# Attention pass of a macaron block: couplings, inverse products and reads in halves of eight heads, slot sums taken out of PSUM, new engine orders with four tiles in flight

## The reference

```
x = x + 0.5 * ffn(layernorm(x))
x = x + attn(layernorm(x))
x = x + 0.5 * ffn(layernorm(x))

attn(x):  q, k = l2norm(x@Wq), l2norm(x@Wk);  v = x@Wv
          a = sigmoid(x@Wa + ba);  b = sigmoid(x@Wb + bb)        # one number per head
          for every token: pred = S^T k;  S = a*S + k (b*(v - pred))^T;  y = S^T q
          return (rmsnorm(y, g_norm) * silu(x@Wg)) @ Wo
ffn(x):   logits = (gelu([x, mean(slots)]@w1.T + b1)@w2.T + b2) / (|tau| + 0.1)
          alpha  = softmax over the 8 greatest of 64 logits, 0 elsewhere
          slots' = GRU(alpha^T x / sum(alpha), slots);  return (alpha @ (slots'@wv.T + bv))@wo.T + bo
```

## Time and profile before

| | |
|---|---|
| median of 3 runs | 3262.46 us (3257.69 to 3265.82) |
| profiled execution, its own time | 3255.6 us |
| its span, first to last instruction | 3253.7 us |
| PE / DVE / POOL / ACT busy | 87% / 60% / 38% / 29% of the span |
| mean granted TensorE clock | 0.94 |
| attention pass begins | about 331.6 us from the span's start |

### The profile page before, as it was taken

How to read it: one execution, slowest core, us unless ns; L and a number is a source line. 1 busy time by engine, 2 the same in 40 slices (tenths; PEclk the granted TensorE clock), 3 DMA queues, 4 the chain that set the end, 5 groups by cost and what they waited for, 6 DMA issues and landing times.

```text
span 3253.7 us, 121458 instructions
## 1 busy us (share of the span) xinstructions
PE 2816.3 (87%) x52828; PEld 1973.8 (61%) x52828; DVE 1939.1 (60%) x5299; ACT 944.0 (29%) x1634; POOL 1232.0 (38%) x1608
## 2 busy tenths in 40 slices
PE   6998778898988888888888888898988898889857
PEld 5786456565666665666666556666666665666643
DVE  6776446565666665666655556565656666655635
ACT  4775122222222222222222222222222222222210
POOL 2221344344444443444444434443444443444400
PEclk9999899999999999999999999999999999999978
DMA  6341122221212222222122221122222222112167
GB/s 207 98 151 48 34 55 56 49 56 30 54 50 56 56 55 56 56 56 56 49 50 56 56 49 44 37 53 56 56 56 56 56 56 56 52 48 56 49 213 287
DMA packets 365983, 225.05 MB, mean 69 GB/s; under 512 B 277584, under 2 KB 294032, under 8 KB 365456
## 3 DMA queue, kind: packets, MB, share of 16 engines
q1 hardware_dynamic: 356240, 200.51, 22.6%
q10 hardware_dynamic: 9216, 16.78, 1.4%
HBM read 125.49 MB, written 74.97 MB: 62 GB/s over the span
## 4 chain that ended last, share of the span: by engine, by line
PE 49%; DVE 32%; issue 10%; DMA 4%; SPq 2%; POOL 1%; ACT 1%; DVEq 0%; POOLq 0%; ACTq 0%
DVE blk L1823 12%; DVE blk L1825 12%; PE psum L784 8%; PE psum L958 5%; PE psum L867 4%; PE psum L938 4%; PE psum L915 4%; PE psum L885 4%; PE psum L925 4%; PE psum L829 3%; DMA xin<-in_L_attn_x_dram 3%; PE psum L852 2%; PE psum L898 2%; PE psum L986 2%; PE psum L778 2%
## 5 line engine op out<-in xcount | busy, mean ns | idle before, releaser
L784 PE MATMUL psum<-w_kvqg,xnT 128*128 128x512 f32 x1536 | 730.7, 609 | 5.2 <-issue 2.0
L1369 POOL TENSOR_TENSOR sm<-sm,half 128x1 f32<-128x1 f32 (+1 forms) x384 | 518.2, 1350 | 476.8 <-DVE sm L1765 198.1
L1823 DVE TENSOR_TENSOR blk<-blk 128x30 f32<-128x30 f32 (+14 forms) x960 | 379.9, 396 | 84.9 <-issue 53.0
L784 PEld LDWEIGHTS psum<-w_kvqg,xnT 128*128 128x128 f32 x1536 | 271.4, 191 | 257.1 <-issue 229.8
L1825 DVE TENSOR_TENSOR blk<-blk 128x30 f32<-128x30 f32 (+14 forms) x960 | 375.8, 391 | 33.0
L1403 POOL TENSOR_SCALAR sm<-sm 128x1 f32<-128x1 f32 x64 | 14.6, 228 | 772.6 <-DVE sm L1733 772.6
L829 PE MATMUL psum<-xnT,w_kvqg 128*128 128x128 f32 x2048 | 300.1, 309 | 0.0
L829 PEld LDWEIGHTS psum<-xnT,w_kvqg 128*128 128x128 f32 x2048 | 289.6, 224 | 17.2 <-issue 17.2
L958 PE MATMUL psum<-w_out,gate 128*128 128x512 f32 x512 | 265.4, 643 | 2.9 <-issue 1.3
L1841 DVE STREAM_TRANSPOSE st<-psum 128x128 f32<-128x128 f32 x256 | 80.9, 316 | 278.2 <-PE psum L938 277.8
L1199 ACT ACTIVATE xn<-xc,sm 128x512 f32<-128x512 f32 x64 | 52.0, 813 | 657.5 <-POOL sm L1407 657.5
(11 more groups left out here) (271 smaller groups left out, 4839.2 us busy)
## 6 DMA issues: line engine op xcount, KB each, us to landing
blk<-n_scratch SPq DMA_DIRECT2D x64, 512.0 KB, 4.9
xin<-in_L_attn_x_dram SPq DMA_DIRECT2D x96, 256.0 KB, 2.9
n_scratch<-nn SPq DMA_DIRECT2D x64, 256.0 KB, 3.3
xh<-xc SPq DMA_DIRECT2D x64, 256.0 KB, 2.5
e_scratch<-blk SPq DMA_DIRECT2D x32, 512.0 KB, 2.6
E<-e_scratch SPq DMA_DIRECT2D x64, 256.0 KB, 4.3
x_scratch<-xh SPq DMA_DIRECT2D x62, 256.0 KB, 4.5
rxn<-in_L_attn_x_dram SPq DMA_DIRECT2D x32, 256.0 KB, 3.1
```

What stands on the lines that cost most here:

```text
L784: last = mm(dst, xnT[b][:, k * P:(k + 1) * P], w_kvqg[:, (k * 4 + m) * D:(k * 4 + m + 1) * D], start=(k == 0), stop=(k == KC - 1))
L1369: return g.tensor_tensor(dst, a, half[:, 0:n], ALU.pow)
L1823: own(tt(o, Y[:, 0:rows, s_:s_ + 1].to_broadcast([P, rows, cols]), N[:, s_:s_ + 1, s_ + 1:CH].to_broadcast([P, rows, cols]), ALU.mult))
```

## The change

All of it is in the attention pass, but for one scaling of Wo.

- **Halves.** `gram`, `coupling`, `reading`, `apply_uw`, `move_uw`, `qe_T`, `apply_gy`, `move_gq` and `chunk_kept` work on halves of eight heads, each half in one PSUM bank of its own. `apply_gy` goes through four pieces of two turns; each turn has 8 products where it had 16, and is awaited before the next on the same bank.
- **Projections.** Value and gate-decay columns stand side by side: `proj_va` takes the 32 columns of Wa and Wb and the first 256 of Wv, `proj_vb` the other 256. `ab` is gone. The values are kept in two places by turns (`vk` has three parts).
- **cum.** 32 products per tile with 4 columns become 4 products with 32 columns; DVE prepares their operand `glx`.
- **Gate.** ScalarE computes Silu at once; before it took Tanh and DVE finished it. The factor 0.5 in `set_out` goes. `y_mean` moves from DVE to ScalarE. The four `max(.,1e-24)` of the norms move from DVE to POOL.
- **Slot sums.** `slots` starts and stops in one bank; ScalarE copies it out (`slot_copy`), POOL adds it to `slotacc` (`slot_add`). Before, a bank of its own summed over all tiles.
- **Orders and depth.** Four tiles are in flight (p, q, r, s), over 35 steps where there were 34. The bank map and all five orders are new. The couplings of a tile are now made in the step after its projections, and inverted in the same step; `apply_uw` of b = 0 ends that step.

The core of the diff:

```diff
-        gram_at = [banks(3, 2), banks(5, 2)]
-        uw_at = [banks(1, 2), banks(4, 2)]
-        gq_at = [banks(4, 2), banks(4, 2)]
-        slot_at = banks(7, 1)
+        slot_at = banks(1, 1)
+        gram_at = [[banks(7, 1), banks(6, 1)], [banks(1, 1), banks(3, 1)]]
+        uw_at = [[banks(7, 1), banks(3, 1)], [banks(1, 1), banks(4, 1)]]
+        gq_at = [[banks(6, 1), banks(5, 1)], [banks(2, 1), banks(5, 1)]]
...
+            def proj_va(n, b):
+                pe.wait_ge(S["xnT"], both(n, b))
...
+                project(b, W_AB, 2 * H + D // 2, va_at[b][:, 0:2 * H + D // 2], range(KC)).then_inc(S["va_ps"], 1)
...
-                for b in range(B):
-                    for h in range(H):
-                        last = mm(q32(cum_at, h % NC, (6 + b) * H + h // NC * NC, NC),
-                                  gla[:, b * H + h:b * H + h + 1].to_broadcast([P, HD]),
-                                  chunk[:, 0:P:CH], start=False, stop=True, skip_group_check=True)
+                for hq in range(NC):
+                    last = mm(q32(cum_at, hq, 6 * H, 2 * H), ones[:, 0:HD], glx[:, hq * 2 * H:(hq + 1) * 2 * H],
+                              start=False, stop=True, skip_group_check=True)
...
+                for r in (2 * (piece % 2), 2 * (piece % 2) + 1):
+                    turn = 2 * NC * (n - 1) + NC * part + r
+                    since(gq_turn[b], turn)
                     stand_alone(pe)
...
+                    for k in range(2):
+                        for c in range(NC):
+                            hq = (c + r) % NC
+                            at = ((2 * part + k) * NC + hq) * 2 * HD
+                            last = mm(q32(gq_at[b][part], hq, (k * NC + c) * 2 * HD, 2 * HD), q32(uw[b], c, at + HD, HD),
+                                      q32(pk[b], c, at, 2 * HD), start=False, stop=True, skip_group_check=True)
+                    last.then_inc(gq_turn[b], 1)
+                    since(y1_turn[b], turn)
...
-            def tanh_g(n, b):
+            def gate_of(n, b):
                 sc.wait_ge(S["g_ps"], both(n, b))
...
+                act(gate[b][:, :], g_at[b], ACT.Silu).then_inc(S["gate"], 1)
...
+            def slot_copy(n):
+                sc.wait_ge(S["slot_ps"], both(n, 1))
+                since(S["sla"], n - 1)
+                act(slt[:, :], slot_at, ACT.Copy).then_inc(S["slc"], 1)
...
             def key_power(n, b):
                 pl.wait_ge(S["ssk"], both(n, b))
+                stand_alone(pl)
+                own(g.tensor_scalar(s(b, "ssk"), s(b, "ssk"), 1e-24, None, ALU.max))
...
+            def slot_add(n):
+                pl.wait_ge(S["slc"], n)
+                since(S["sla"], n - 1)
+                g.tensor_tensor(slotacc[:, 0:D], slotacc[:, 0:D], slt[:, :], ALU.add).then_inc(S["sla"], 1)
```

More of the change, by code:

```diff
@@ L119, in build @@
         gt = sb("gt", 28 * H)
+        slt = sb("slt", D)
+        glx = sb("glx", NC * B * H)
+        vk3 = [vk[b][:, :].rearrange("p (m h e) -> p m h e", m=3, h=H) for b in range(B)]
         def heads(t, n=1):
@@ L542, in drain_loads @@
             def drain_loads():
-                sp.wait_ge(y1_turn, NC * both(NT, 1))
+                for b in range(B):
+                    sp.wait_ge(y1_turn[b], 2 * NC * NT)
                 for g in range(3):
@@ L790, in proj_k @@
                     pe.wait_ge(S["xnT"], both(n, b))
-                    if b == 1:
-                        free((n, (S["zi"], n)))
-                last = project(b, 0, k_at[b], part)
+                    if b == 0:
+                        free((n - 2, (S["yv"], both(n - 2, 1))), (n - 1, (T["pt"][0], nth(n - 1, 0))))
+                    else:
+                        free((n - 2, (S["top"], both(n - 2 + NT, 0))), (n - 1, (S["vb"], both(n - 1, 1))))
+                last = project(b, W_K, D, k_at[b], (2 * part, 2 * part + 1))
                 if part == 1:
@@ L944, in y_norm @@
                 if b == 0:
-                    free((n, (S["qg"], both(n, 1))))
+                    free((n, (S["ysq"], both(n, 0))))
                 else:
@@ L1487, in step_pool @@
                     y_power(r, 1)
-                if p is not None:
-                    first_rstd(p, 0)
+                if q is not None:
+                    query_decayed(q, 0)
+                if s is not None:
+                    slot_add(s)
                 if r is not None:
@@ L1785, in key_turn @@
             def key_turn(n, b):
-                since(S["gram_ps"], both(n - 1, b))
+                since(T["gram_ps"][b], 2 * (n - 1))
                 ve.wait_ge(S["kn"], both(n, b))
@@ L1952, in step_dve @@
-                if q is not None:
-                    second_sum(q, 0)
-                    state(q, 1, 2)
-                    last_moments(q, 0)
-                    state(q, 1, 3)
-                    gated(q, 1)
-                if p is not None:
-                    coupling(p, 1)
+                    gates_beta(p)
             ve.wait_ge(wih_st, RELOAD)
```

900 lines of the change are left out of this document (476 added, 424 removed).

## The result

| | before | after |
|---|---|---|
| median, same chip | 3264.14 us (3257.69 to 3268.61, 4 runs) | 3332.66 us (3330.19 to 3355.88, 4 runs) |
| ratio | | **1.0235** (1.0206 to 1.0265) |
| profiled execution's own time, and its span | 3255.6, 3253.7 us | 3330.19, 3328.4 us |
| mean granted clock | 0.94 | 0.934 |
| step of the pass | 86.7 us | 88.3 us |

What follows compares the result with a forecast made beforehand. PE was taken to bound the kernel: 71.2 us work plus 4.3 us new waits make a 75.5 us step. 3255.6 - 31 x (86.7 - 75.5) + 13 for head and tail gave 2920 us; 8-in-10 range 2800 to 3065.

Steps and rivals of the forecast that it cites:

- Step of 86.7 us, and its split: One step on PE before the change: 10.0 us idle, at most 4.3 lost to low clock, 72.4 work.
- the wait of `logits`: PE's `logits` waits for `xc` from `first_sum(p,1)`, behind DVE's inversion: 4.97 us a step, half the idle time.
- the low clock with the gap: PE's 1.2 GHz level behind the `logits` gap, 4.4 us, claimed to go when that gap goes.
- Turns of `apply_gy` are half as long ... I take +0.3 (0 to 1): PE's shorter `apply_gy` turns: 0 to 0.06 us in each of 16 turns, +0.3 us a step taken.
- The work of 71.2 us: PE's full-clock work per new step: 72.4 - 1.3 (`ab`) - 0.35 (`cum`) + 0.3 (turns) + 0.2 (mode changes).
- The waits that go: On PE, the 4.97 us gap of `logits` and the low clock behind it go, barring a new gap that long.
- Waits that come: Four late places in the new order: 0.7, 0.6, 1.3 and 1.7 us, adding 4.3 us a step on PE.
- `uw` for `kn`: PE's `uw(r,1,0)` waits for `kn` because POOL's `key_power(q,1)` is late: 0.7 us a step.
- `first_sum(p,0)` holding the ring: DVE's `first_sum(p,0)` waits inside the inversion for `hold(q,0)`: 3 us in the ring, 1.7 us on PE at `chain(r,1,2)`.
- The ring of 70.4 us: Loop of PE work, couplings, DRAM trip, DVE inversion and inverse's return: 70.4 us, 74.7 with waits, just under PE's 75.5.
- The rival "slower": Loop through DVE, POOL, ScalarE and SP's queue over 11.6 us late, at `first_sum(p,0)`: 3300 us; chance 0.06.
- My own test: Signs of being wrong on PE include clock staying at 0.95 or `apply_gy` turns taking over 0.6 us.

Runs made afterwards that it cites:

- b1: Kernel before with `first_sum` and `first_moments` of b = 1 moved from behind the inversion to its middle: 3324.52 us, ratio 1.0153.
- a6: Kernel after without the counter increments in its apply products, waits kept: 3076.75 us, ratio 0.9397 to the kernel before.
- m4_which: TensorE alone, sets of 128 small and 6 big products, waits and increments varied separately: 10.8 us a set with 16 waits, 14.0 with 16 increments.
- m1_supply: TensorE alone, small products unbroken or alternating with big ones, some beside DRAM copies: unbroken, 1.99 us of work, then 1.5 to 1.7 us of nothing.
- m3_cover: TensorE alone, six stretches varying hand-overs and the products between them: full turns 11.0 us a set, halves 15.3, no hand-over 11.2.
- m2_turns: TensorE alone, small products with and without loads beside them, and sets in full or half turns: 10.5 us a set full, 15.6 in halves.

## Why the prediction was wrong

- **Step of 86.7 us, and its split: read rightly,** but the idle 10.0 us were then treated as if they were the wait of `logits` and small change. Of them 4.1 us are pauses inside runs of small products, released by nothing. They were there to be read in the kernel before, and no part of the change takes them away: even without the increments 3.9 us a step are left. To give back the low clock with the gap was nearly right: of the 38 stretches at the low level between 700 and 3000 us, 26 lie behind a wait of `logits`, with 195 of 235 us. What I took for nothing is the low clock behind other pauses, and these grew.
- **"Turns of `apply_gy` are half as long ... I take +0.3 (0 to 1)": the step that failed.** The hand-over itself was priced well (the half turns without increments cost 86.4 - 85.8 = 0.6 us a step in the kernel before). What I didn't count is that every turn carries an increment, so that 14 a step become 32. The half turns as they stand cost 96.6 - 86.7 = 9.9 us a step in the kernel before, where I took 0.3 and at most 1. In the kernel after the increments cost 88.3 - 80.4 = **7.9 us a step**: idle 2.4, low clock 2.8, and 2.7 of what the split calls work. The rows show a part of this last: at the full clock a pair of half turns takes 0.61 us with increments (1586.94 to 1587.55) and 0.51 without (1555.80 to 1556.31), 1.6 us for the 16 pairs of a step.
- **The work of 71.2 us: right but for the increments.** With them it is 74.0, without them 71.3. So `ab` into the value projection, `cum` and the mode changes were sized well together; none was tried alone.
- **"The waits that go": right** for `logits`. That the place of `first_sum(p,1)` isn't enough, b1 showed.
- **"Waits that come": 4.3 us a step in sum as I gave them, some 2 in the profile.** `ffn` for `aT_in`: 11.4 us in the whole run (32.5 in a6), where I had 1.3 a step. `uw` for `kn`: none. `first_sum(p,0)` holding the ring: `chain(r,1,2)` doesn't wait for it. In its place `proj_va(p,0)` waits for `second_sum(r,1)`, 36.0 us, 1.2 a step, which I hadn't listed. `chain` for `st`: 11.2 us in all (0.5 a step forecast). The ring of 70.4 us doesn't lead in any kernel with the new orders: PE waits for `E` once, for 8 to 10 us in the whole run.
- **What remains of the gap.** The kernel after without the increments takes 80.4 us a step, where I had 75.5: 3.2 us more idle (pauses of 3.9 that I hadn't counted) and 1.6 us of low clock. That would have been 0.9397 x 3262, some 3065 us, at the edge of the range. The sum of both is the miss: 31 x (7.9 + 4.9) = 397 us, and 12 more in head and tail, which came to 25 us where I had 13.
- **The rival "slower" came true for another reason:** no loop of DVE and SP was late. My own test, "turns of `apply_gy` over 0.6 us" and "the clock stays at 0.95", both say wrong, the first only behind the pauses: a pair of half turns (32 instructions, as a turn before) took 0.60 us, and 0.82 at the low clock.

What isn't settled: why an increment that nobody waits for makes the next packet of instructions start later. It isn't their share of what is delivered: a6 has 407 packets where the kernel after has 410. The trace shows no time for an increment on PE. Shown is that with increments in the run the packet starts later, the pause is longer by about as much, and the clock is lower. With 32 increments in a set of m4_which it is otherwise: the packet starts 0.6 us ahead, the pauses are shorter than with 16 (2.0 against 2.7 us, medians), and TensorE is busy longer with the same products (86.83 us instead of 77.22, at about the same clock).

## What to carry to other kernels

Count everything that a loop's turn carries, not only its products: cutting turns in half more than doubled the bare semaphore instructions in TensorE's densest stretch, and these cost more (7.9 us a step) than the wait that the new order removed (5.6). In a profile, sum the waits with releaser "issue" first: no semaphore ends them, so moving other engines' work doesn't give them back, and they can grow. Compare them with the starts of the instruction packets in the DMA records. Where a short experiment with the engine alone reproduces the pause, take its instructions out one kind at a time.

## What the runs showed of the hardware

- Small products (32x32, 64 columns) alone: 64 of them (128 instructions, with as many weight loads) in 1.99 us, one such block every 3.46 to 3.73 us (m1_supply). In alternation of 32 small with two products of 512 columns: no pause.
- Each such pause belongs to one packet of 16 KB in the instruction queue; TensorE goes on 1.4 us (median) after its landing and 2.3 to 2.6 us after its start, in m1_supply, m3_cover, m4_which and the kernels alike.
- One counter increment to each 8 products: a set of 128 small and 6 big products takes 14.0 us instead of 11.2 without (m3_cover), with two increments in each place 14.7 (m4_which). A satisfied wait costs nothing that can be told (10.8). The packet starts at the beginning of the pause instead of some 1.2 us ahead of it.
- Behind pauses of at most 1.7 us the clock stayed at 0.98 on average (m4_which, waits alone); with pauses of up to 3.0 us, in the stretch with increments, it was 0.88; the bare half turns, with pauses of at most 1.5 us, had 0.96.
- Loads of 512 KB beside small products lengthened a block from 3.5 to 4.8 us at a DMA share of 0.52 (m2_turns, one execution, clock 0.74 beside them and 1.00 without).
